# Sums of exponentials in an attention kernel: GpSimd adds all eight tiles, VectorE a quarter of the first addition, with six tile buffers

## The reference

```python
xn = group_norm(x, gamma, beta)                       # 32 groups of 8 channels
qkv = einsum('bchw,oc->bohw', xn, w_qkv) + b_qkv      # 8 heads of 32 channels
m = softmax(einsum('bhcs,bhct->bhst', q * scale, k * scale), axis=-1)
a = einsum('bhst,bhct->bhcs', m, v)
return x + einsum('bchw,oc->bohw', a, w_proj) + b_proj
```

## Time and profile before

| | |
|---|---|
| time, median of three runs | 2117.92 us (2113.89 to 2124.2) |
| time of the profiled execution | 2112.97 us |
| its span, first to last instruction | 2111.2 us |
| busy: PE, DVE, ACT, POOL | 98%, 80%, 59%, 85% |
| additions on GpSimd (L876) | 381, of which 64 are a half's first |
| matmul records of the sums (L451) | 536 of tiles `pt`, 512 of `acc` |

### The profile page before, as it was taken

One profiled execution on the slowest core, in us unless ns is written; L12 is line 12 of the kernel. 1 busy time (PEld: TensorE's weight loads), 2 busy tenths in 40 slices (PEclk: granted clock), 3 DMA queues, 4 the chain that ended last, 5 costly groups with the idle time before them and its releaser, 6 DMA issues.

```text
span 2111.2 us, 31126 instructions
## 1 busy us (share of the span) xinstructions
PE 2073.6 (98%) x10552; PEld 1148.2 (54%) x10552; DVE 1698.3 (80%) x2896; ACT 1248.4 (59%) x2321; POOL 1790.4 (85%) x567
## 2 busy tenths in 40 slices
PE   6999999999999999999999999999999999999998
PEld 3455555555555555555555555555555555556542
DVE  5888888888888788888888888888888888887881
ACT  2556666565665656656565565655656566566563
POOL 2688888898898898888898888988988988888995
PEclk9999999999999999999999999999999999999998
DMA  4342233432224332234422334322243322333210
GB/s 127 61 101 55 54 74 81 101 76 58 64 66 101 81 89 48 59 88 101 101 56 57 75 81 101 76 77 51 60 101 81 94 42 61 86 81 81 58 41 23
DMA packets 208668, 156.45 MB, mean 74 GB/s; under 512 B 166528, under 2 KB 166784, under 8 KB 208512
## 3 DMA queue, kind: packets, MB, share of 16 engines
q1 hardware_dynamic: 207936, 152.91, 32.1%
q10 hardware_dynamic: 576, 1.57, 0.3%
HBM read 36.39 MB, written 16.78 MB: 25 GB/s over the span
## 4 chain that ended last, share of the span: by engine, by line
PE 93%; POOL 4%; DVE 1%; ACT 1%; issue 0%; DMA 0%; SPq 0%; ACTq 0%; POOLq 0%; DVEq 0%
PE ps_t L391 24%; PE ps_m L416 21%; PE ps_v L437 21%; PE ps_d L459 10%; PE ps_m L451 6%; PE ps_d L474 5%; PE ps_d L467 5%; POOL acc L876 3%; DVE raw_max L708 1%; ACT pt L626 1%; PE ps_m L467 0%; PE ps_m L459 0%; PE ps_t L482 0%; DMA par<-pars_dram 0%; ACT xn L658 0%
## 5 line engine op out<-in xcount | busy, mean ns | idle before, releaser
L626 ACT ACTIVATE pt<-ps_t 128x512 f32<-128x512 f32 x2048 | 1121.9, 599 | 799.0 <-PE ps_t L391 783.5
L708 DVE TENSOR_REDUCE raw_max<-ps_m 128x1 f32<-128x512 f32 x2048 | 1336.6, 686 | 294.4 <-PE ps_m L416 292.2
L876 POOL TENSOR_TENSOR acc<-acc,pt 128x2048 f32<-128x2048 f32 x317 | 1450.4, 4576 | 43.9 <-ACT pt L626 1.6
L416 PE MATMUL ps_m<-ks,qs 96*128 96x512 f32 x2048 | 985.8, 482 | 9.3 <-DVE raw_max L708 7.0
L391 PE MATMUL ps_t<-qs,ks 97*128 97x512 f32 x2048 | 841.8, 412 | 5.7 <-ACT pt L626 3.5
L391 PEld LDWEIGHTS ps_t<-qs,ks 97*128 97x128 f32 x2048 | 389.4, 190 | 369.9 <-issue 219.6
L437 PE MATMUL ps_v<-pt,v 128*32 128x512 f32 x4096 | 494.2, 599 | 0.0
L416 PEld LDWEIGHTS ps_m<-ks,qs 96*128 96x128 f32 x2048 | 388.3, 190 | 178.7 <-DVE raw_max L708 106.2
L876 POOL TENSOR_TENSOR acc<-pt 128x2048 f32<-128x2048 f32 x64 | 293.2, 4581 | 221.7 <-ACT pt L626 221.7
L459 PE MATMUL ps_d<-xn,wq 128*128 128x512 f32 x500 | 256.8, 596 | 5.7 <-ACT xn L658 5.7
L437 PEld LDWEIGHTS ps_v<-pt,v 128*32 128x32 f32 x4096 | 116.4, 109 | 256.9 <-issue 179.2
(11 more groups left out here) (49 smaller groups left out, 533.4 us busy)
## 6 DMA issues: line engine op xcount, KB each, us to landing
qs<-stage_qh SPq DMA_DIRECT2D x256, 128.0 KB, 2.4
ks<-stage_kh SPq DMA_DIRECT2D x248, 128.0 KB, 2.4
qs<-stage_ql SPq DMA_DIRECT2D x128, 128.0 KB, 2.4
qs<-neg_max SPq DMA_DIRECT2D x1024, 0.5 KB, 2.0
ks<-stage_kl SPq DMA_DIRECT2D x124, 128.0 KB, 2.4
xn<-x_dram SPq DMA_DIRECT2D x16, 512.0 KB, 4.2
res<-x_dram SPq DMA_DIRECT2D x16, 512.0 KB, 4.7
between<-res SPq DMA_DIRECT2D x32, 256.0 KB, 2.3
```

The source lines that it names most:

```text
L416: pe.matmul(ps_m[max_bank(u)][:, :], qs[b][0:KROWS, h, c:c + P], ks[b][0:KROWS, h, kf * HALF:(kf + 1) * HALF], start=True, stop=True).then ...
L626: act.activation(pt[t % 4][:, h, :], ps_t[score_bank(s.g, u)][:, :], ACT.Exp, scale=SCALE).then_inc(exp_done, 1)
L708: dve.tensor_reduce(raw_max[:, e % 2, t, kf:kf + 1], ps_m[max_bank(u)][:, :], AX.X, ALU.max)\
L876: pool.tensor_tensor(acc[hf][:, :, :], a[:, :, :], pt[t % 4][:, :, :], ALU.add).then_inc(pool_added, 1)
```

## The change

GpSimd now adds all eight tiles in each half but the last (`POOLED` 8 for 7), so that TensorE's sums take `acc` alone. VectorE adds one head of four of the first addition (`add_quarter`, after its maximum at unit 9 of the half), and GpSimd the three others; GpSimd waits for VectorE's part before its second addition. There are six buffers `pt` for four, taken by turns over all halves. A matrix `ident` that nothing used is no longer loaded. `LAST_PIECES` has the value 2 that `CT` had in its places.

```diff
-POOLED = 7
+POOLED = 8
+TILES = 6
+QUARTER_AT = 9
-        pt = [sb(f"pt{b}", [P, HG, HALF]) for b in range(4)]
+        pt = [sb(f"pt{b}", [P, HG, HALF]) for b in range(TILES)]
+        def tile_of(half, t):
+            return pt[(NT * half + t) % TILES]
-            sp.dma_start(ident[:, :], ident_in).then_inc(loaded, 16)
@@ sums (PE)
                 pe.wait_ge(pool_added, ADDS * half + pooled - 1)
+                tiles = [tile_of(half, t) for t in range(pooled, NT)] + [acc[hf]]
-                tiles = [pt[t % 4] for t in range(pooled, NT)] + [acc[hf]]
@@ exp (ACT)
-                if h == 0 and started:
-                    act.wait_ge(pv_done, NT * half + t - 3)
-                    if t >= 4:
-                        act.wait_ge(pool_added, ADDS * half + max(1, t - 4))
-                    elif t + 4 < POOLED:
-                        act.wait_ge(pool_added, ADDS * (half - 1) + t + 4)
-                    else:
-                        act.wait_ge(sum_ready, half)
+                before = NT * half + t - TILES
+                if h == 0 and before >= 0:
+                    act.wait_ge(pv_done, before + 1)
+                    old, k = divmod(before, NT)
+                    act.wait_ge(pool_added, ADDS * old + max(1, k))
+                    if k < 2:
+                        act.wait_ge(quarter_added, old + 1)
@@ new (DVE)
+            def add_quarter(half):
+                dve.wait_ge(exp_done, HG * (NT * half + 2))
+                if half >= NH:
+                    dve.wait_ge(sum_ready, half - 1)
+                dve.tensor_tensor(acc[half % NH][:, HG - 1, :], tile_of(half, 0)[:, HG - 1, :],
+                                  tile_of(half, 1)[:, HG - 1, :], ALU.add).then_inc(quarter_added, 1)
+                    if u % (UNITS // NH) == QUARTER_AT:
+                        add_quarter(NH * s.n + u // (UNITS // NH))
@@ add (POOL)
-                pool.tensor_tensor(acc[hf][:, :, :], a[:, :, :], pt[t % 4][:, :, :], ALU.add).then_inc(pool_added, 1)
+                heads = slice(0, HG - 1) if t == 1 else slice(0, HG)
+                if t == 2:
+                    pool.wait_ge(quarter_added, half + 1)
+                pool.tensor_tensor(acc[hf][:, heads, :], a[:, heads, :], tile_of(half, t)[:, heads, :],
+                                   ALU.add).then_inc(pool_added, 1)
```

More of the change, by code:

```diff
@@ L147, in dense_at, with attention_layers @@
     return step, int(part > 0)
-def attention_layers(nc, x, w_qkv, w_proj, pars, bias_v, bias_proj, ident_in, group_in, out):
+def attention_layers(nc, x, w_qkv, w_proj, pars, bias_v, bias_proj, group_in, out):
     nc.disable_value_cache = True
@@ L170, in attention_layers @@
         bp = sb("bp", [P, CT])
-        ident = sb("ident", [P, P])
         group = sb("group", [P, P])
@@ L238, in attention_layers @@
         pool_added = sem("pool_added")
+        quarter_added = sem("quarter_added")
         sum_ready = sem("sum_ready")
@@ L437, in weighted_values @@
                     mm = pe.matmul(ps_v[HD * h:HD * (h + 1), :], v[s.v][:, t, c:c + HD],
-                                   pt[t % 4][:, h, :], start=(t == 0), stop=(t == NT - 1))
+                                   tile_of(half, t)[:, h, :], start=(t == 0), stop=(t == NT - 1))
                 mm.then_inc(pv_done, 1)
@@ L530, in dense @@
                     project_qk(s.g, 1 - s.v, r, part)
-                elif not has_next and LAST_OUT <= step < LAST_OUT + CT:
+                elif not has_next and LAST_OUT <= step < LAST_OUT + LAST_PIECES:
                     piece = step - LAST_OUT
@@ L561, in slot @@
                         group_stats(s.j + 2, ps_t[stats_bank()])
-            pe.wait_ge(loaded, 32)
+            pe.wait_ge(loaded, 16)
             group_stats(0, ps_v)
@@ L597, in _ @@
             sums(last, NH - 1, UNITS * SLOTS, sums_bank(0), POOLED_LAST)
-            for piece in range(CT, CT * NH):
+            for piece in range(LAST_PIECES, CT * NH):
                 pe.wait_ge(proj_done, 4 * (BLOCKS - 1) + piece)
@@ L612, in exp @@
                 half = NH * s.n + half_of
-                started = not (isinstance(half, int) and half == 0 and t < 4)
-                if h == 0 and started:
-                    act.wait_ge(pv_done, NT * half + t - 3)
-                    if t >= 4:
-                        act.wait_ge(pool_added, ADDS * half + max(1, t - 4))
-                    elif t + 4 < POOLED:
-                        act.wait_ge(pool_added, ADDS * (half - 1) + t + 4)
-                    else:
-                        act.wait_ge(sum_ready, half)
+                before = NT * half + t - TILES
[5 more added lines that the diff above has]
+                        act.wait_ge(quarter_added, old + 1)
                 act.wait_ge(st_ready, UNITS * s.n + u + 1)
-                act.activation(pt[t % 4][:, h, :], ps_t[score_bank(s.g, u)][:, :], ACT.Exp, scale=SCALE).then_inc(exp_done, 1)
+                act.activation(tile_of(half, t)[:, h, :], ps_t[score_bank(s.g, u)][:, :], ACT.Exp, scale=SCALE).then_inc(exp_done, 1)
             def values_out(half):
@@ L785, in slot @@
                             v_out(s.j + 1, 1 - s.v, step)
-                    if part == 1 and not has_next and LAST_OUT <= step < LAST_OUT + CT:
+                    if part == 1 and not has_next and LAST_OUT <= step < LAST_OUT + LAST_PIECES:
                         project_out(s.j, step - LAST_OUT)
@@ L870, in add @@
                         pool.wait_ge(sum_ready, half - 1)
-                    a = pt[0]
+                    a = tile_of(half, 0)
                 else:
@@ L905 @@
 LAST_OUT = 5
+LAST_PIECES = 2
 _OUT = (B, C, 32, 32)
@@ L939 @@
                                     for b in (L0_conv_b_proj, L1_conv_proj_b)]),
-        "ident_dram": np.eye(P, dtype=np.float32),
         "group_dram": np.kron(np.eye(P * GROUPS // C), np.full((C // GROUPS,) * 2, GROUPS / C / QUARTERS)).astype(np.float32),
```

## The result

The changed kernel takes 2204.36 us (median of four runs, 2199.2 to 2208.98) beside 2115.9 us of the kernel before in the same comparison: ratio 1.041, 95% interval 1.039 to 1.043. It is slower by 88 us. The median forecast was 2194, with 2188 to 2214 as the forecast's own range. The profiled execution takes 2208.98 us, 96 more than that of before, where 78 were forecast.

A forecast was written before the change was run, and what follows sets the result against it. GpSimd was taken to become the bound: start 69.73 us, 63 halves of 31.75, 14 group norms of 2.77, quarters 43.5 and 37.3 at the end give span 2189.6, profiled 2191.4, median 2194; range 2188 to 2214.

The forecast's parts named there:

- The bound: Middle halves: GpSimd becomes the bound, 31.75 us a half, 129.8 in four with group norm; TensorE needs 124.4.
- The price of exclusion: VectorE's quarter against GpSimd's additions: between nothing and 0.69 us a half; upper bound taken, 43.5 us in all.
- rival B: At the quarter: GpSimd always first at the lock, 0.93 us a half, 2206, median 2211; counted within the forecast's 0.68.
- both engines meet at GpSimd's period: With GpSimd first: late division takes TensorE's half up to 35.1 us, but the stall shrinks as GpSimd finishes ahead.
- GpSimd's inputs come in time: Units 4 to 7 are ready for its first addition; unit 31 is some 6 us past before its seventh.
- Rival C: TensorE loses its clock in the new waits and becomes the bound again: 2240 likelier, 2287 at most; chance 0.06.
- The sum: Whole program: last half's first addition at 2152.3 us plus 37.3 after it, span 2189.6, 78.4 more than before.
- The marks: Expected trace signs: no GpSimd idle before first additions, busy 95% or more, chain mostly through it, TensorE waiting 0.6 to 2 us.
- B's mark: Sign of GpSimd being first at the lock: VectorE idle 3 us or more before its quarter, and a late division.
- the sign of being wrong in the main point: GpSimd having idle time left in the middle of the program would refute it as the bound.
- Buffers and `ident` at nothing: Six buffers worth at most ScalarE's 6.9 us of waits, inside GpSimd's time anyway; dropping the ident transfer worth nothing.

The follow-up runs named there:

- run 2: The changed kernel with VectorE's quarter replaced by a sum over the same slice of tile 1, one SBUF input, same waits and signals: 2156.01 us, ratio 1.019.
- run 1: The changed kernel without VectorE's quarter, GpSimd adding all four heads of all eight tiles, six buffers kept: 2221.24 us, ratio 1.050.
- run 3: The changed kernel with POOLED back to 7, so GpSimd adds seven tiles; VectorE's quarter and the six buffers stay: 2171.7 us, ratio 1.027.
- run 9: The changed kernel with TensorE doing three extra sets of tile 7 products before the sums after a group norm's half: 2223.7 us, ratio 1.050.
- run 6: The changed kernel with POOLED = 7 and no quarter, leaving only the six buffers and the dropped ident load: 2114.88 us, ratio 0.998.
- run 4: The changed kernel without the quarter, GpSimd adding eight tiles in each slot's first half and seven in its second, six buffers: 2102.23 us, ratio 0.994.
- run 8: The changed kernel without the quarter, eight and seven tiles by turns up to half 59, then 7, 7, 5 and 4: 2096.16 us, ratio 0.990.

## Why the prediction was right

**The bound.** GpSimd's half was sized from the spacing of starts. Run 2 gives 129.76 us for four halves beside 129.8, run 1 gives 32.8 beside 28.15 + 4.70 = 32.85. This step is right to a tenth of a microsecond, and recorded durations would have missed it.

**The price of exclusion.** It is real (runs 2 and 3), but 0.69 us a half was a choice and not a measured size, and the halves show two prices. Where VectorE is first, GpSimd loses 0.45: 32.2 us a half. Where GpSimd is first, it waits 0.72 for the quarter and then for the exponentials, and a half takes 33.2 to 33.8, 1.5 to 2.0 over the 31.75. The mean is 51.4 / 63 = 0.82. I had the second case as rival B, priced at 0.93 a half, with the claim that both engines meet at GpSimd's period. That claim is the step that failed: I held that GpSimd's inputs come in time, and had looked at its first and its seventh addition; the exponentials for the third come 1.0 to 1.6 us late, because three things stand behind one another (quarter, maxima, exponentials). Nor does the stall shrink by itself: three such halves follow one another. Over the program the difference is (133.17 - 132.53) x 15.5 = 10 us.

**TensorE's clock.** Rival C had it as the whole of a slower case. It does occur, after each group norm's half that finds TensorE early, in the timeline:

```profile
1141.74 1.52 PE L456 MATMUL ps_m<-acc,ones 128*32 128x512 f32 x8 [2.89 <-POOL acc L896]
```

and in windows of 2 us after it:

```profile
1142.00:1144.00 2.00, 2.00 (x16) 0.54 (x12) 2.00 (x4) 0.00 (x0) 2.00 (x1) 0.55 0.11 43
1144.00:1146.00 2.00, 2.00 (x16) 0.30 (x8) 1.83 (x5) 0.00 (x0) 1.87 (x2) 0.59 0.96 250
```

After 2.89 us of waiting the clock is at the 1.2 GHz level for most of 4 us. With 0.79 over 8 us TensorE has lost some 1.7 us, and VectorE comes to its next quarter 32.5 us after GpSimd's first addition (1141.65 to 1174.16), where the quick group has 31.2 (1010.12 to 1041.32). The clock alone does not make TensorE the bound, as the prediction said and run 2 shows, but it hands GpSimd the lock in the next three halves. That link was not foreseen.

**The sum.** 2189.6 us of span were forecast. Measured are 2206.9: 8.7 more at the start, 9.7 more from the first addition to that of the last half (2170.70 - 78.41 = 2092.3, forecast 2082.6), and 1.1 less after it. The start was no term of the forecast, and the runs do not tie it to the change.

**What was luck.** The sign is not luck: without any exclusion GpSimd's halves alone made the kernel slower, and run 2, without it, is slower by 1.9%. That the time lies in the forecast's range is in part. The range's top was rival B with its low price, and only about three halves in eight went that way. In run 9, where all groups behind the filler are slow, the time is 2223.7 us, outside the range.

**The marks.** GpSimd without idle time ahead of its first additions is there. Busy at 95% of the span is not: it is 92%, since GpSimd is busy for 12.6 us of the first 78.4 and for 12.5 of the last 36.2, where the mark counted the whole span; from the first addition to that of the last half it is 1999.1 of 2092.3 us, 95.5%. TensorE idle ahead of the sums by 0.6 to 2 us is there only in quick halves, with 0.7 to 0.8. B's mark, VectorE idle for 3 us ahead of its quarter, could not have shown B: that wait is recorded inside the quarter (3.95 us at 1174.16). And the sign of being wrong in the main point, idle time of GpSimd in the middle, is there in part, the 12.9 and 28.2 us above: none of it stands before a first addition, and it is the quarter's consequence, but in those halves GpSimd is not the bound by itself. The chain was to run through GpSimd for most of the program and has 31%; TensorE needs 31.1 of 32.2 us and so may take much of a chain though it sets little, which is argued and not shown. Buffers and `ident` at nothing: run 6 agrees.

## What to carry to other kernels

Before an engine is given more work, put its half (or period) beside the one that sets the pace, by the spacing of starts and with all of its rarer work; here 129.8 us against 127.9 settled the sign. Work cut in pieces that fit is worth more than work moved whole: the added tile in every other half, without the quarter, made the kernel 0.6% faster (run 4), and 1.0% with fewer additions at the end (run 8). And an addition of two operands in SBUF on VectorE is to be kept away from GpSimd's long additions, also where GpSimd has time left (run 3, busy for 108 of 131.5 us); if it must be, what is queued behind the instruction decides the price, more than its length.

## What the runs showed of the hardware that was not expected

Where a VectorE addition of two SBUF operands and a GpSimd addition exclude one another, the wait is recorded as the instruction's own duration, on VectorE (0.76 to 3.97 us for one shape in the changed kernel) and on GpSimd (3.93 in place of 3.48), and not as idle time with a releaser; a spread of durations within one shape is its mark. With one SBUF input, 64 operations of VectorE under a full GpSimd took 674 to 686 ns. When VectorE is first, a GpSimd addition that is queued loses 0.45 us and not the quarter's 0.7; why it is less is open.
